# Softmax-bound preparation spread over more units of the attention loop: a pause between square and matmul, and a tail cut in three

## What is computed

```
mod = silu(c) @ wmod                      -> sa, ca, ga, sb, cb, gb
h = layernorm(x) * (1 + ca) + sa
q, k, v = h @ Wq + bq, h @ Wk + bk, h @ Wv + bv
attn = softmax(q k^T / sqrt(128))         per head, over 4096 keys
out  = attn @ v1 - lam * attn @ v2        v1, v2: the two halves of v's heads
x = x + ga * (0.2 * layernorm(out) @ Wo + bo)
h = layernorm(x) * (1 + cb) + sb
x = x + gb * (gelu(h @ w1 + b1) @ w2 + b2)
```

## Time and profile before

| | |
|---|---|
| two timed runs | 3297.85 and 3472.78 us, median 3385.32 us |
| profiled execution | 3298.4 us |
| its span on the slowest core (core 1) | 3296.8 us |
| spans of the eight cores | 3287.6 to 3296.8 us |
| PE busy | 2696.0 us (82%) |
| ACT busy | 1658.3 us (50%) |
| DVE busy | 779.7 us (24%) |
| the attention loop on core 1 | first exponential at 773.48, last block from 1917.98 us |

### The profile page before, as it was taken

How to read it: one execution, slowest core, us unless ns; L and a number is a source line. 1 busy time by engine, 2 the same in 40 slices (tenths; PEclk the granted TensorE clock), 3 DMA queues, 4 the chain that set the end, 5 groups by cost and what they waited for, 6 DMA issues and landing times.

```text
span 3296.8 us, 50219 instructions; the slowest of 8 cores (3287.6 to 3296.8 us)
## 1 busy us (share of the span) xinstructions
PE 2696.0 (82%) x19760; PEld 1585.5 (48%) x19760; DVE 779.7 (24%) x1606; ACT 1658.3 (50%) x2273; POOL 271.3 (8%) x288
## 2 busy tenths in 40 slices
PE   3467787776989898998989973773599999999998
PEld 0223333333656565655656642231456666565665
DVE  0132222335130403223130025581111010111101
ACT  0034333004989898988989987352223323232331
POOL 1000111120000000000000000461000010000001
PEclk9978888887999999999999985896899999999999
DMA  6621221221010110101010014468601010010100
GB/s 94 112 74 60 70 70 34 69 84 30 8 33 8 33 37 8 33 8 36 8 33 8 11 46 106 140 217 157 109 33 45 27 46 33 33 46 26 52 27 26
DMA packets 93164, 175.26 MB, mean 53 GB/s; under 512 B 49923, under 2 KB 49923, under 8 KB 89862
## 3 DMA queue, kind: packets, MB, share of 16 engines
q0 software_dynamic: 25920, 88.09, 11.4%
q1 hardware_dynamic: 67014, 83.95, 8.9%
HBM read 151.05 MB, written 58.72 MB: 64 GB/s over the span
## 4 chain that ended last, share of the span: by engine, by line
PE 49%; ACT 24%; DVE 10%; DMA 7%; issue 7%; SPq 3%; DVEq 0%; POOLq 0%; ACTq 0%; POOL 0%
ACT expT L790 21%; PE pu L1268 14%; PE py L1296 13%; PE pdn L581 7%; PE qk L781 3%; SPq L49 3%; DVE nrow L731 3%; PE pv L547 2%; DMA x_scr<-x_sb 2%; PE pv L551 2%; DMA wmod_sb<-wmod 2%; DVE bnd L736 2%; PE avA L808 1%; DVE sq_scr L717 1%; ACT deadout L888 1%
## 5 line engine op out<-in xcount | busy, mean ns | idle before, releaser
L790 ACT ACTIVATE expT<-qk,Bneg 128x1024 bf16<-128x1024 f32 x1024 | 1047.1, 1147 | 115.8 <-PE qk L781 114.2
L781 PE MATMUL qk<-qT,kT 128*128 128x512 bf16 x2048 | 614.9, 384 | 24.6 <-ACT expT L790 23.8
L1279 ACT ACTIVATE g_sb<-pu,b1pT 128x256 bf16<-128x256 f32 x512 | 242.7, 474 | 611.0 <-PE pu L1268 611.0
L1268 PE MATMUL pu<-h2T,w_sb 128*128 128x256 bf16 x4096 | 452.4, 272 | 1.6 <-ACT h2T L1251 1.3
L1296 PE MATMUL py<-w_sb,g_sb 128*128 128x512 bf16 x2048 | 444.6, 379 | 0.0
L1268 PEld LDWEIGHTS pu<-h2T,w_sb 128*128 128x128 bf16 x4096 | 367.0, 97 | 87.7 <-issue 2.2
L808 PEld LDWEIGHTS avA<-v_aug,expT 128*128 128x128 bf16 x3072 | 254.8, 98 | 256.1 <-issue 30.1
L808 PE MATMUL avA<-v_aug,expT 128*128 128x129 bf16 x3072 | 345.0, 222 | 12.8 <-ACT expT L790 12.8
L808 PE MATMUL avB<-v_aug,expT 128*128 128x129 bf16 x3072 | 346.5, 222 | 0.0
L1296 PEld LDWEIGHTS py<-w_sb,g_sb 128*128 128x128 bf16 x2048 | 199.8, 98 | 237.8
L808 PE MATMUL avC<-v_aug,expT 128*128 128x129 bf16 x2048 | 286.9, 222 | 0.2 <-DVE ao_ch L848 0.2
(11 more groups left out here) (192 smaller groups left out, 1882.4 us busy)
## 6 DMA issues: line engine op xcount, KB each, us to landing
x_tiles<-x SPq DMA_DIRECT2D x64, 512.0 KB, 4.3
x_scr<-x_sb POOLq DMA_DIRECT2D x32, 512.0 KB, 5.1
w_sb<-w POOLq DMA_DIRECT2D x8, 2048.0 KB, 58.6
x1f<-x_scr SPq DMA_DIRECT2D x16, 1024.0 KB, 6.0
out<-x2st SPq DMA_DIRECT2D x32, 512.0 KB, 2.6
wmod_sb<-wmod POOLq DMA_DIRECT2D x24, 512.0 KB, 5.4
qT_scr<-qstg POOLq DMA_DIRECT2D x64, 128.0 KB, 2.5
kT_scr<-qstg POOLq DMA_DIRECT2D x64, 128.0 KB, 2.7
```

Of the source, the lines that this page charges most:

```text
L781: p.emit("tensor", lambda e, pp=pp, kt=kt, qc=qc, half=half, qT=qT, kTs=kTs: e.matmul(qk_ps[pp][:, half * 512:(half + 1) * 512], kTs[:, kt ...
L790: p.emit("scalar", lambda e, pp=pp, ppe=ppe, h=h: e.activation(expT[:, ppe * QCW:(ppe + 1) * QCW], qk_ps[pp][:, :], AF.Exp, scale=ISQ, bia ...
L1268: p.emit("tensor", lambda e, ppu=ppu, mt=mt, kt=kt, ppb=ppb: e.matmul(p_u[ppu][:, :], w1_sb[:, kt * FF + mt * 128: kt * FF + (mt + 1) * 12 ...
L1279: p.emit("scalar", lambda e, ppu=ppu, mt=mt: e.activation(g2_sb[:, mt * SBW:(mt + 1) * SBW], p_u[ppu][:, :], AF.Gelu, bias=b1pT[:, mt:mt + ...
```

## The change

`prep_units` gets three more `yield`s, and so ten more steps: one between each square and its first matmul (eight), one between Exp and the matmul that spreads the bound, one between that matmul and the copy `Bneg`. No instruction is added, dropped or altered, and no wait.

```diff
@@ -720,6 +720,7 @@
                     src_[:, c4 * 1024:(c4 + 1) * 1024]), waits=sqdep, inc="dve")
                 sqn = ("dve", p.n("dve"))
                 yield
+                yield
                 for c2 in range(2):
                     cid = c4 * 2 + c2
                     p.emit("tensor", lambda e, c2=c2, sq_half=sq_half: e.matmul(
```

## The result

The changed kernel took 3258.78 us in the median of seven runs, the kernel before 3299.27 us in six beside them. The ratio is 0.9876, with a 95% interval of 0.9863 to 0.9889: 1.2% or 40 us faster, clear of noise and under the 2% bound. The forecast was 3250 us, a gain of 48.8.

The account below looks back on a forecast made before the run. ScalarE's exponentials bound the loop, with TensorE late through interleaved preparation. Per head 3.42 + 2.2 + 1.8 = 7.4 us instead of 14.4, over seven heads a gain of 48.8: 3250 us, range 3219 to 3279.

Parts of the forecast that it names:

- the most that can be won: Interleaved preparation of the next head in seven heads of the loop: costs 100.8 us in all, 3.1%.
- the 134.66 us: Time of the last head's four blocks, which prepare no next head; preparing heads took 149.06 us each.
- Part 1, undisturbed pairs: Square's two matmuls away from a block's end: 0.57 us per pair, six pairs 3.42 us per head, no wait for the square.
- the first rival (everything hides): Pairs of preparation matmuls cost nothing, 3.0 us per head left, gain 80, 3219 us; chance 0.10.
- the second rival: PE's wait for the square comes back: 11.3 us per head, gain 22, 3277 us; chance 0.13.
- Part 1, the block's end: End of a head's first block: late evacuation delays square and matmul of unit 34; 2.2 us per head.
- Part 2, the tail: Ln, Exp, spreading matmul and `Bneg` ending each preparation: 1.8 us per head after the change, Ln's wait being next.
- the 14.4: Microseconds the interleaved preparation cost per preparing head before the change; forecast to fall to 7.4.
- The clock rule: Idle gaps lower PE's clock and the first work after runs slow; a shorter wait after Ln and Exp would spare such units.
- The slower rival: PE at its lower clock through some 34 preparation units: 25.6 us per head, +78 us, 3377 us; chance 0.04.
- the 18: Lower-clock units per head, at 0.70 us lost each, from which the change would stop being a gain.

Follow-up runs that it names:

- the first edit alone: Against the kernel before, only the added unit between each square and its first matmul, with Ln, Exp, spreading matmul and `Bneg` left in one unit; ratio 0.989.

## Why the prediction was right, and where it was off

**What bounds the kernel, and the most that can be won.** Right. The whole difference is in the seven preparing heads (39.1 of 39.6 us), and no experiment moved anything outside them that the traces could tell: the rest of the slowest core's span is 2253 us before and after, and 2246 to 2257 us in the other runs, in no order that follows the edits. The four blocks in the 134.66 us are the last of head 6 and the first three of head 7, none of which holds a step, so the number stands.

**Part 1, undisturbed pairs.** Right: 0.58 to 0.62 us measured for 0.57, six times. The first pair of a head, read from the trace before, was the right stand-in for a pair without a wait; the first rival (everything hides) had no pair that cost nothing. PE no longer waits for the square there, with DVE's 4.31 us under the four units' 4.62, so the second rival fell as well. (Its price was a little high: six undisturbed pairs at 1.0 are 6.0, not 7.0, which gives 3270 us and not 3277.)

**Part 1, the block's end.** The step that failed in size: "and 0.37 for the pair's second matmul: 2.0. With the 0.20 the block's end costs 2.2." It measured 3.56 in the slower form and 1.4 less where PE kept its clock; there the head took 141.97 us, 0.1 from the forecast. The sequence was right. What the step left out is that behind PE's waits there (0.93, 0.23, 0.18 and 0.63, or 1.97 us of the 3.3 up to 959.29) the lower level comes in most heads, as behind the longer wait of the tail. I had seen that behaviour in the earlier trace rows and said of the clock only that the change would spare it. The change took the fall away from the tail (42 of 56 heads, then none) and left it at the block's end (43, then 46), where it now costs 1.4 us and had cost 0.5 to 0.9. The step was read from head 6, one of the two heads of core 1 in which the clock had held there. On that core the clock had cost 1.2 us per head at the tail and 0.5 at the block's end in the mean; the forecast counted the whole 1.7 as won, and 1.4 came back. Seven heads by 1.4 us are 9.8 us, the 9.7 by which the forecast of the loop (48.8) exceeds the trace (39.1). That it fits so closely is in part luck: six pairs cost 0.2 us more than forecast and the tail 0.1 less.

**Part 2, the tail.** Right: 1.66 for 1.8, with Ln's 0.66 us of waiting next in line, which the experiment with Ln a unit later took away. The price of the tail before was put at the mean of all heads within the 14.4, so its clock losses, and those of the block's end before, were in the 14.4 although the steps named neither.

**The clock rule.** The Trainium skill ("TensorE: Matmul & The Clock Gate", HAM oscillation) describes a kernel whose PE waits for a DMA ahead of every tile and starts each tile at the lower clock. The waits there are longer than any here, so the trace agrees in kind only: PE runs slow behind idle at both places, with a granted clock of 0.61 behind the block's end on core 7, though its longest single wait there is 0.93 us. The 0.99 of the earlier trace rows did not show the fall behind the tail, since that window ends at 1724.00 and most of the slow stretch lies behind it (granted 0.65 from 1724 to 1727). I used the rule where it favoured the change and not at the block's end, where my own steps had a new cluster of gaps. That was the mistake.

**The slower rival.** Its mechanism is real, its size was not: one to two units per head run at the lower level, far from the 18 at which it would have decided.

## What to carry to other kernels

Side work put into a busy engine's queue costs the part of its own time that the loop cannot hide plus each wait in front of it: read both from the trace, the first from a place where the input was ready long before. Spread it one instruction per unit, have each producer two units ahead, and leave out the stretch in which the pipeline drains and fills; here that gave 2.3% where the change gave 1.2%. When an edit moves idle time of TensorE, list the new gaps as well as the old ones, and look at the clock behind the same place in every head and on every core: here one head showed it held, and most did not.

## What the runs showed of the hardware

The fall of the clock is not tied to the gap alone. With the same order and the same four waits at the block's end, head 1 took 141.97 us on core 0 and 143.38 on core 7; on core 4 two heads of seven kept the clock, on core 0 two, in all 10 of 56. With the first edit alone 53 of 56 heads kept it, and the four waits are the same to 0.02 us in all 112 heads of the two kernels. With the idle partly filled, it held there in all 56. What decides in between is not settled by these runs. Adding 1.1 us of needless matmuls per head made the head 1.3 us shorter on the slowest core.
